# Layer 1's linear attention: one raw projection of queries and keys, with the four taps moved from TensorE to ScalarE, GpSimd and VectorE

## The reference, cut to what matters

```python
def short_conv(x, w):                       # w: 128 channels x 4 taps
    xp = jnp.pad(x, ((0, 0), (3, 0), (0, 0)))
    y = x
    for j in range(4):
        y = y + xp[:, j:j + l, :] * w[:, j]
    return y
q = l2norm(silu(short_conv(x @ Wq.T, conv_q)))      # 16 heads of 8
k = l2norm(silu(short_conv(x @ Wk.T, conv_k)))
v = silu(short_conv(x @ Wv.T, conv_v))
# per head: o = q @ W_init + causal(q @ k.T) @ v, normalised over the head's 8 channels
return (layernorm(o) * gamma + beta) * (x @ Wg.T) @ Wo.T
```

## Time and profile before

| | us |
|---|---|
| median of 3 runs (3835.6 to 3837.76) | 3836.73 |
| the profiled execution | 3835.66 |
| its span in the profile | 3833.8 |
| TensorE matmul busy over the span | 3465.1 (90%) |
| VectorE busy | 2688.0 (70%) |
| ScalarE busy | 2437.2 (64%) |
| GpSimd busy | 2075.0 (54%) |

### The profile page before, as it was taken

One profiled execution on the slowest core, in us unless ns is written; L12 is line 12 of the kernel. 1 busy time (PEld: TensorE's weight loads), 2 busy tenths in 40 slices (PEclk: granted clock), 3 DMA queues, 4 the chain that ended last, 5 costly groups with the idle time before them and its releaser, 6 DMA issues. The chain is left out here.

```text
span 3833.8 us, 90102 instructions
## 1 busy us (share of the span) xinstructions
PE 3465.1 (90%) x30069; PEld 2574.1 (67%) x30069; DVE 2688.0 (70%) x5870; ACT 2437.2 (64%) x9595; POOL 2075.0 (54%) x2606
## 2 busy tenths in 40 slices
PE   8989979988988999999889998899899998788897
PEld 5656645557776878888666665666688874456587
DVE  6857749977774767777688886644577754979822
ACT  6958944445452437777635991455688875688655
POOL 4534319977993433344366540275666635556744
PEclk9989999999999999999989998999999999999889
DMA  7013420010000000000000003135500003300078
GB/s 110 2 23 48 53 61 1 1 56 1 1 1 22 2 2 7 6 7 6 6 2 6 12 7 119 28 99 91 220 22 21 22 30 116 116 2 10 31 263 302
DMA packets 320103, 185.17 MB, mean 48 GB/s; under 512 B 214104, under 2 KB 289127, under 8 KB 318613
## 3 DMA queue, kind: packets, MB, share of 16 engines
q1 hardware_dynamic: 303716, 147.68, 14.2%
q0 software_dynamic: 13568, 27.36, 3.1%
q10 hardware_dynamic: 2370, 4.39, 0.3%
HBM read 131.43 MB, written 50.54 MB: 47 GB/s over the span
## 5 line engine op out<-in xcount | busy, mean ns | idle before, releaser
L3889 POOL DMA_INDIRECT l2f_b_xb<-l2f_tokens,l2f_inv x160 | 155.5, 972 | 174.8 <-issue 157.9
L2684 POOL TENSOR_TENSOR l1x_Sx<-l1x_Sx,l1x_sm 128x512 f32<-128x512 f32 x128 | 132.6, 1046 | 184.7 <-DVE l1x_sm L2890 184.7
L2684 POOL TENSOR_TENSOR l3a_Sx<-l3a_Sx,l3a_sm 128x512 f32<-128x512 f32 x128 | 133.4, 1043 | 129.8 <-DVE l3a_sm L2890 128.2
L3005 ACT ACTIVATE l1x_Sx<-l1x_Sx,l1x_nmx 128x128 f32<-128x128 f32 x512 | 199.0, 393 | 3.8 <-DVE l1x_nmx L2884 3.8
L1470 PEld LDWEIGHTS l0f_acc<-l0f_d_xk,l0f_d_Z 128*128 128x128 f32 x1024 | 124.7, 191 | 113.8 <-POOL l0f_d_Z L1438 112.8
L3005 ACT ACTIVATE l3a_Sx<-l3a_Sx,l3a_nmx 128x128 f32<-128x128 f32 x512 | 199.0, 392 | 0.1
L865 ACT ACTIVATE l3f_Pr<-l3f_S,l3f_nmx 128x128 f32<-128x128 f32 x512 | 182.5, 402 | 3.3 <-DVE l3f_nmx L795 3.3
L865 ACT ACTIVATE l2x_Pr<-l2x_S,l2x_nmx 128x128 f32<-128x128 f32 x512 | 183.9, 426 | 0.4 <-DVE l2x_nmx L795 0.4
L1350 ACT ACTIVATE l0x_Pr<-l0x_S,l0x_nmx 128x128 f32<-128x128 f32 x512 | 181.4, 403 | 3.1 <-DVE l0x_nmx L1267 2.6
L865 ACT ACTIVATE l0a_Pr<-l0a_S,l0a_nmx 128x128 f32<-128x128 f32 x512 | 182.6, 406 | 0.7 <-DVE l0a_nmx L795 0.7
L1470 PE MATMUL l0f_acc<-l0f_d_xk,l0f_d_Z 128*128 128x128 f32 x1024 | 144.5, 284 | 25.1 <-POOL l0f_d_Z L1438 24.9
(11 more groups left out here) (757 smaller groups left out, 11938.7 us busy)
## 6 DMA issues: line engine op xcount, KB each, us to landing
l3f_b_W<-in_l3f_we SPq DMA_DIRECT2D x72, 514.0 KB, 5.5
l3f_sorted<-l3a_blank SPq DMA_DIRECT2D x1, 17680.0 KB, 51.1
l3x_Mb<-l3x_dram_max SPq DMA_DIRECT2D x32, 512.0 KB, 4.3
l2f_results<-l2f_b_ys SPq DMA_DIRECT2D x40, 256.0 KB, 2.8
l2f_W<-in_l2f_w SPq DMA_DIRECT2D x1, 6144.0 KB, 25.9
l3f_b_xb<-l3f_sorted SPq DMA_DIRECT2D x72, 65.0 KB, 4.4
l0f_ew<-in_l0f_ew SPq DMA_DIRECT2D x1, 4096.0 KB, 13.2
l3f_XS<-l3f_results SPq DMA_DIRECT2D x8, 512.0 KB, 6.6
```

The lines of the kernel that those rows point to most:

```text
L2684: pool.tensor_tensor(quad(Sx, s, q), quad(Sx, s, q), bcast_in(sm[:, s, 4 * q:4 * q + 4], P), ALU.mult).then_inc(w_done, 1)
L3005: ins = nc.scalar.activation(Sx[:, s, h, :], Sx[:, s, h, :], ACT.Exp, bias=nmx[:, s, h:h + 1], accum_out=sm[:, s, h:h + 1])
L3889: pool.indirect_dma_start(xb[:, j % 16, :], None, rows[:, :], bass.IndirectOffsetOnAxis(inv[:, j:j + 1], 0), bounds_check=None).then_inc(x ...
```

## The change

The queries and keys are projected once, raw, by one matmul each, from the unshifted block. ScalarE then reads each result from PSUM four times, scaling by a per-channel column (`cols[:, n, j]`, the tap) and writing at a shift of 3-j tokens to `terms`: eight activations for each block, four for the queries (`scale_terms(b, 0)`) and four for the keys (`scale_terms(b, 1)`). GpSimd adds terms 0 and 1 to terms 2 and 3 in one instruction of 128x512 (`pair_terms`); VectorE adds the two halves in one of 128x256 (`convolve`); and `silu_qk` reads the sum from SBUF. Values and gate are projected as before. The pipeline becomes deeper: LayerNorm runs for b+6, `apply` for b+5, `normed_T` and `copy_normed` for b+4, the projection for b+3, and the loop over steps begins at -6. `xb` has three buffers, and bank A comes free at `scaled`. A small DMA brings the tap columns `l1a_cc`, and one small VectorE instruction adds 1 to the last tap.

```diff
-    xb = sb("xb", [P, 2, 3 + P])
+    xb = sb("xb", [P, 3, 3 + P])
+    terms = sb("terms", [P, 4, 2, P])
+    cv = sb("cv", [P, 2, 2, 2, P])
...
+        def pair_terms(b):
+            wait(pool, scaled, b + 1)
+            wait(pool, qkt_done, b - 1)
+            if b == 0:
+                wait(pool, zeros_done, 1)
+            pool.tensor_tensor(cv[:, b % 2, :, :, :], terms[:, 0:2, :, :], terms[:, 2:4, :, :],
+                               ALU.add).then_inc(pairs_done, 1)
...
             if span(b - 2):
                 gated(b - 2)
-            if span(b + 4):
-                wait(pool, ln.done, b + 3)
-                ln.rstd(pool, b + 4, b % 2, C)
-                ln.offset(pool, b + 4, b % 2)
+            if span(b + 3):
+                pair_terms(b + 3)
+            if span(b + 6):
+                wait(pool, ln.done, b + 5)
+                ln.rstd(pool, b + 6, b % 2, C)
+                ln.offset(pool, b + 6, b % 2)
...
         def project_qk(b, n):
-            wait(pe, xb_done, b + 1)
-            wait(pe, qkt_done, b)
+            wait(pe, xb_done, min(b + 2, NB))
+            wait(pe, scaled, b)
             if b == 0:
                 wait(pe, zeros_done, 1)
-            cols = slice(n * P, (n + 1) * P)
-            for j in range(4):
-                mm = nc.tensor.matmul(A[:, cols], taps[:, j, cols], xb[:, b % 2, j:j + P],
-                                      start=(j == 0), stop=(j == 3))
+            mm = nc.tensor.matmul(A[:, n * P:(n + 1) * P], (wq, wk)[n], xb[:, b % 3, 3:3 + P], start=True, stop=True)
...
         def normed_T(b):
             wait(pe, ln.done, b + 1)
-            wait(pe, qkt_done, b)
+            wait(pe, scaled, b - 1)
...
             if span(b - 2):
                 turn_scale(b - 2)
+            if span(b + 4):
+                normed_T(b + 4)
             if span(b - 1):
                 sum_keys(b - 1)
-            if span(b + 2):
-                project_qk(b + 2, 0)
+            if span(b + 3):
+                project_qk(b + 3, 0)
             if span(b - 1):
                 centre(b - 1)
-            if span(b + 2):
-                project_qk(b + 2, 1)
+            if span(b + 3):
+                project_qk(b + 3, 1)
...
-            if span(b + 3):
-                normed_T(b + 3)
...
+        def convolve(b):
+            wait(dve, pairs_done, b + 1)
+            nc.vector.tensor_tensor(cv[:, b % 2, 0, :, :], cv[:, b % 2, 0, :, :], cv[:, b % 2, 1, :, :],
+                                    ALU.add).then_inc(conv_done, 1)
...
                 mask(b, 1)
-            if span(b + 4):
-                wait(dve, ln.offset_done, b + 3)
-                ln.moments_of(nc, dve, b + 4, b % 2, X)
+            if span(b + 2):
+                convolve(b + 2)
+            if span(b + 6):
+                wait(dve, ln.offset_done, b + 5)
+                ln.moments_of(nc, dve, b + 6, b % 2, X)
...
+        def scale_terms(b, n):
+            wait(act, qk_mm, b + 1)
+            wait(act, pairs_done, b)
+            if b == 0:
+                wait(act, zeros_done, 1)
+            for j in range(4):
+                ins = nc.scalar.activation(terms[:, j, n, 3 - j:P], A[:, n * P:n * P + P - 3 + j], ACT.Identity,
+                                           scale=cols[:, n, j:j + 1])
+            if n == 1:
+                ins.then_inc(scaled, 1)
...
         def silu_qk(b):
             wait(act, pv_mm, b - 3)
             wait(act, qexp_done, b - 3)
-            wait(act, qk_mm, b + 1)
-            nc.scalar.activation(qkT[:, b % 4, :], A[:, 0:2 * P], ACT.Silu).then_inc(qkt_done, 1)
+            wait(act, conv_done, b + 1)
+            nc.scalar.activation(qkT[:, b % 4, :], cv[:, b % 2, 0, :, :].rearrange("p n t -> p (n t)"), ACT.Silu).then_inc(qkt_done, 1)
...
         def copy_normed(b):
-            wait(act, vg_mm, b - 1)
+            wait(act, vg_mm, b - 2)
...
             if span(b - 2):
                 copy_scale(b - 2)
-            if span(b + 3):
-                ln.apply(nc, act, b + 3, (b + 3) % 2, X, xnt_mm)
+            if span(b + 4):
+                copy_normed(b + 4)
+            if span(b + 5):
+                ln.apply(nc, act, b + 5, (b + 1) % 2, X, xnt_mm)
...
                 square_centred(b - 1)
+            if span(b + 3):
+                scale_terms(b + 3, 0)
             if span(b + 2):
                 silu_qk(b + 2)
                 silu_v(b + 2)
             if span(b + 3):
-                copy_normed(b + 3)
+                scale_terms(b + 3, 1)
...
+                sp.dma_start(cc[:, :, :], d["l1a_cc"]).then_inc(w_in, 16)
...
-                dve.wait_ge(w_in, 64)
+                dve.wait_ge(w_in, 80)
+                nc.vector.tensor_scalar(cc[:, :, 3], cc[:, :, 3], 1.0, 0.0, ALU.add, ALU.add)
```

More of the change, by code:

```diff
@@ L1904, in stage_l0_ffn, with delta_attention @@
         combine_slots(nc, C, sems, "l0f_c", X, XT, phiX, val)
-def delta_attention(nc, C, sems, x, tag, X, taps, wg, woT, w0, affine):
+def delta_attention(nc, C, sems, x, tag, X, wq, wk, cols, taps, wg, woT, w0, affine):
     sb = lambda n, shape: x.enter_context(nc.sbuf_tensor(f"{tag}_{n}", shape, F32))
     ln = LayerNorm(nc, sb)
-    xb = sb("xb", [P, 2, 3 + P])
+    xb = sb("xb", [P, 3, 3 + P])
+    terms = sb("terms", [P, 4, 2, P])
+    cv = sb("cv", [P, 2, 2, 2, P])
     qkT = sb("qkT", [P, 4, 2 * P])
@@ L1931, in delta_attention @@
      v_done, qexp_done, s_mm, p_done, pv_mm, ot_done, cen_mm, osq_done, rt_mm, rt_done, u_done,
-     wide_done, g_done, y_mm, x_done) = sems(27)
+     wide_done, g_done, y_mm, x_done, scaled, pairs_done, conv_done) = sems(30)
     ln.sems(sems)
@@ L2035, in project_v @@
             for j in range(4):
-                nc.tensor.matmul(B[:, 0:P], xb[:, b % 2, j:j + P], taps[:, j, 2 * P:3 * P],
+                nc.tensor.matmul(B[:, 0:P], xb[:, b % 3, j:j + P], taps[:, j, 2 * P:3 * P],
                                  start=(j == 0), stop=(j == 3))
-            nc.tensor.matmul(B[:, P:2 * P], wg, xb[:, b % 2, 3:3 + P], start=True, stop=True).then_inc(vg_mm, 1)
+            nc.tensor.matmul(B[:, P:2 * P], wg, xb[:, b % 3, 3:3 + P], start=True, stop=True).then_inc(vg_mm, 1)
         def normed_T(b):
             wait(pe, ln.done, b + 1)
-            wait(pe, qkt_done, b)
+            wait(pe, scaled, b - 1)
             nc.tensor.transpose(A[:, 2 * P:3 * P], ln.xn[:, b % 2, :], C.ident).then_inc(xnt_mm, 1)
@@ L2129, in vector @@
         nc.vector.memset(xb[:, :, 0:3], 0.0)
+        nc.vector.memset(terms[:, 0:3, :, 0:3], 0.0)
         nc.vector.memset(Vx[:, :, :], 0.0).then_inc(zeros_done, 1)
@@ L2171, in copy_normed @@
         def copy_normed(b):
-            wait(act, vg_mm, b - 1)
+            wait(act, vg_mm, b - 2)
             wait(act, xnt_mm, b + 1)
-            nc.scalar.copy(xb[:, b % 2, 3:3 + P], A[:, 2 * P:3 * P]).then_inc(xb_done, 1)
+            nc.scalar.copy(xb[:, b % 3, 3:3 + P], A[:, 2 * P:3 * P]).then_inc(xb_done, 1)
         def step(b):
@@ L2194, in delta_attention @@
                  gpsimd=gpsimd, tensor=tensor, vector=vector, scalar=scalar, S=S, x_done=x_done,
-                 banks={"S0": ((p_done, 2 * NB - 1),), "S1": ((p_done, 2 * NB),), "A": ((qkt_done, NB), (xb_done, NB)),
+                 banks={"S0": ((p_done, 2 * NB - 1),), "S1": ((p_done, 2 * NB),), "A": ((scaled, NB), (xb_done, NB)),
                         "B": ((vs_done, NB),), "O": ((ot_done, NB), (x_done, NB)), "Y": ((u_done, NB), (rt_done, NB), (osq_done, NB), (r_done, NB + 2))})
@@ L3140, in stage_l1_l2_attns @@
         gb = sy("l1a_gb", [P, 2])
+        cc = sy("l1a_cc", [P, 2, 4])
         with nc.psum_tensor("l1a_idle", [P, 512], F32) as idle, nc.psum_tensor("l1x_pb", [P, 512], F32) as pb, \
@@ L3192, in stage_l1_l2_attns @@
         at = len(sems.used)
-        delta = delta_attention(nc, C, sems, y, "l1a", X, taps, w1[:, 3, :], w1[:, 4, :], w0, gb)
+        delta = delta_attention(nc, C, sems, y, "l1a", X, w1[:, 0, :], w1[:, 1, :], cc, taps, w1[:, 3, :], w1[:, 4, :], w0, gb)
         delta_sems = sems.used[at:]
@@ L3222, in _ @@
                 steps = delta.gpsimd(pool), wide.gpsimd(pool), phi.gpsimd(pool), heads.gpsimd(pool)
-                for n in range(-4, HEADS + NB + 2):
+                for n in range(-6, HEADS + NB + 2):
                     steps[0](n)
@@ L3249, in _ @@
                 hold_clock(nc, C, delta.S, 3)
-                for n in range(-3, HEADS + NB + 2):
+                for n in range(-6, HEADS + NB + 2):
                     steps[0](n)
@@ L3301, in _ @@
                 steps = delta.scalar(act), wide.scalar(act), phi.scalar(act), heads.scalar(act)
-                for n in range(-4, HEADS + NB + 1):
+                for n in range(-6, HEADS + NB + 1):
                     steps[0](n)
@@ L4634, in arrange @@
     a["l1a_conv"] = np.concatenate([v["L1_attn_conv_" + n] for n in "qkv"]).T.reshape(-1)
+    a["l1a_cc"] = cols([v["L1_attn_conv_" + n].reshape(P, 4) for n in "qk"])
     blocks = np.zeros((16, 8, 16, 8), np.float32)
```

## The result

| | before | after |
|---|---|---|
| median, us (lowest to highest, runs) | 3837.24 (3835.6 to 3838.83, 4) | 3907.09 (3903.55 to 3909.99, 4) |
| profiled execution, its span | 3835.66, 3833.8 | 3909.99, 3908.2 |
| GpSimd busy over the span | 2075.0 (54%) | 2117.6 (54%) |
| ScalarE busy over the span | 2437.2 (64%) | 2503.3 (64%) |

The changed kernel is slower: ratio 1.018, 95% interval 1.0168 to 1.0193. The forecast of 3881 was 26 us short, and 3907.09 lies above the range's 3903.

A forecast was written before the change was run, and what follows sets the result against it. A new ring ScalarE-GpSimd-ScalarE was to set the block at 8.26 us. Fill 29.0, 26 blocks 214.8, then 6.8 and three of 6.4 sum to 269.8 against 224.3: 45.5 us more, so 3881 us, range 3855 to 3903.

The forecast's parts named there:

- The ring from ScalarE's end through `pair_terms`, LayerNorm and `apply`: New ring of one block, ScalarE to GpSimd and back to ScalarE's last term: 8.26 us, between 7.5 and 8.7.
- the first part: From ScalarE's last term to `apply`: hand-overs 0.06 each, `pair_terms` 1.33, LayerNorm's four 1.41; in all 2.86 us.
- the next ring, through normed_T: `normed_T(b+4)` behind turn_scale waits for the previous step's last terms, with sum_keys queued behind it: 6.9 us.
- The removed matmuls: Queries' and keys' projection on TensorE: 1.33 us a block saved, of which only 0.59 could reach the end.
- matrix work sets the block: Rival: TensorE decides, not the rings; 29 blocks x 1.33 = 39 less, fill 5 more: 3802 us, chance 0.04.
- The rival in which LayerNorm's wait doesn't bind: Offsets are ready earlier, the 6.9 us ring decides, the fill adds 3 to 5: 3840 us, chance 0.06.
- The terms: ScalarE's four activations with one column each, read from PSUM: 1.14 us a run, bounds 0.70 and 1.6.
- The estimate of 1.26 for four: Skill page's figure for four terms on ScalarE, 0.29 each, giving a ring of 8.4; the forecast used 1.14 instead.
- the clock: TensorE: PE busy about three quarters of each block, wait of some 1.5 us for copy_out, 2.4 GHz expected.
- a rival, with half of the blocks slow: Half of the blocks at 1.2 GHz, squares to gate doubled: 16 x 1.8 = 29 more, 3910 us; fallen clock's chance 0.08.
- the fill: Stage's start: first terms at about 6, both groups 8.2, steps -2 to 0 of 6.5 each, Silu table 1.28: 29.0 us.
- `convolve` "costs nothing": VectorE, between mask and moments: some 0.4 us, covered by 1.50 us of idle ahead of `add`.

The follow-up runs named there:

- e2: The changed kernel with LayerNorm's four instructions ahead of `pair_terms` on GpSimd instead of behind it: 3852.31 us, ratio 1.0044.
- e7: The changed kernel with one activation for the keys' terms in place of four from block 1 on: 3871.33 us.
- e3: The kernel before with one projection matmul in place of four for queries and for keys, nothing put in their place: 3819.31 us, ratio 0.9952.
- e1: The changed kernel with idle matmuls in TensorE's waits, five behind the queries' projection and one behind the keys': 3891.96 us, ratio 1.0143.
- e4: The changed kernel with the keys' four terms ahead of `silu_v` on ScalarE instead of behind it: 3865.82 us, ratio 1.0082.
- e5: The changed kernel with LayerNorm's four ahead of `pair_terms` on GpSimd and the keys' terms ahead of `silu_v` on ScalarE: 3862.52 us, ratio 1.0069.
- e6: The changed kernel with two idle matmuls behind the queries' projection and none behind the keys': 3900.63 us.
- e9: e5 with the pairs issued a step later on GpSimd, behind `unit_keys`, where VectorE masks: 3832.8 us, ratio 1.0.
- e8: e5 with one Silu activation on a single column in the setup, to load the table early: 3858.11 us, ratio 1.0056.
- e10: The kernel before with an unused 128x512 addition on buffers of its own ending GpSimd's step: 3856.6 us.
- e11: e10 with a `memset` of 128x1024 in place of the addition: 3834.66 us.

## Why the prediction was wrong, by its steps

- **The sign and the mechanism were right.** The ring from ScalarE's end through `pair_terms`, LayerNorm and `apply` sets the block: 8.36 against 8.26, each of its five parts within 0.10. Inside the first part LayerNorm's four took 1.55 us against 1.41, and the pairs 1.23 up to LayerNorm's start against 1.33. Taking LayerNorm out of it (e2) gives 6.88, where the forecast had the next ring, through normed_T, at 6.9; shortening the terms (e7) shortens the block by as much.
- **The removed matmuls** were worth 0.59 a block, as put (e3). With that the rival "matrix work sets the block" falls: 5.6 us was reached by no kernel. The rival in which LayerNorm's wait doesn't bind falls with e2.
- **The terms** took 1.16 for four (forecast 1.14), the pairs 1.28 alone (1.33). The estimate of 1.26 for four, from the Trainium skill's page "ScalarE: Activation LUTs", section "What ACT_TABLE_LOAD costs", was further off; the measurement decides.
- **The step that failed is the clock:** "My blocks are busier than both, so I expect 2.4 GHz." At full clock they had PE busy for 6.40 of 8.36 us, and the granted clock still fell to half behind the waits, over and over: 0.88 over 25 blocks, 16.1 us, removed by e1 with nothing but idle matmuls. The forecast itself named a clock below 1.00 as a sign that it was wrong. It held this as a rival, with half of the blocks slow, at 3910 and a chance of 0.08; 3907 was measured. That time is nearly the measured one by luck: the price was too high, 29 us against 16.1 (16 times 1.8, where 15 falls cost 1.1 each), by about as much as other terms were too low. Its chance was far too small. The two windows of the earlier trace rows that it went by are of this stage's tail and of layer 3, with the waits laid out in another way, and a mean over a window says nothing of where in it the waits lie.
- **Two terms were mis-sized:** the ring by 0.10 us a block and two somewhat longer blocks, 209.4 - 206.5 = 2.9 by e1's 25 blocks; the fill by 2.1 (39.4 against 37.3). With the clock, 16.1 + 2.9 + 2.1 = 21.1 of the 26 us. At the end of the stage nothing was lost. Of the remaining 5, 1.6 are the profiled execution of before against its median (3837.24 - 3835.66); the other 3 were not placed, and single executions differ by as much ahead of the stage and behind it.
- **`convolve` "costs nothing"** holds in the changed kernel, where VectorE idles 2.73 us ahead of `add`, more than the 1.50 of the earlier trace rows, and even in e2, where it takes 0.93 us and 0.73 of idle time are left. But the forecast looked for room in time only, and not for what GpSimd does meanwhile. In the changed kernel that was harmless (L2117 keeps its 0.17 us); in e4 and e5 `pair_terms` fell on the roots and cost a block 1.0 us.

What stays open: what exactly makes the granted clock fall. e1's filling held it, a third of it in e6 did not. The length of the waits alone does not sort the kernels: in e5 TensorE waited 1.10 us for the roots and 0.20 for square in blocks of 7.50, and the clock stayed at 1.00; in e7 it waited 1.13 us for copy_out and 0.20 for square in blocks of 7.56, and had 0.93. No run tells the two apart.

## What to carry to other kernels

Ahead of moving work onto an engine, write down each queue in order and ask what is queued behind the new instruction's wait: here four tiny instructions behind a 1.28 us addition closed a ring worth 37 us, and a swap undid it. Then look at what the new instruction runs beside: on VectorE's roots it cost 1.0 us a block, beside the mask nothing. Look up first what the removal alone is worth on the present ring (0.59 us a block, not 1.33); the pipeline's extra steps cost their 8 us once, against some 12 won in e9. And once a block has waits on TensorE, price a fallen clock and give it more than a small chance: of the kernels here whose TensorE waits for about 1 us or more in most blocks, the changed one, e6 and e7 lost the clock, e4, e5 and e8 did not.

## What the runs showed of the hardware

- **GpSimd holds some of VectorE's instructions.** Beside a 128x512 addition of two streams on GpSimd, a 128x16 instruction of two SBUF inputs took 1.21 us instead of 0.18 and ended 0.04 us behind it (e5; back at 0.18 in e9, where the addition lies elsewhere). A TENSOR_SCALAR with one SBUF input took 0.64 instead of 0.18 (e10), and 0.45 beside a memset (e11). In these the held instruction ends as GpSimd's ends, so its price is the rest of GpSimd's instruction; the 128x256 `convolve` ended 0.28 us behind (e2). The Trainium skill, page "GPSIMD Engine Reference", section "8. Key points", says that GpSimd shares its SBUF interfaces with VectorE and contends with VectorE's instructions in a 2-port mode or with two SBUF inputs; e5's rows agree, and for the one-input L2094 no row shows which mode it ran in.
- **Others run beside it at their own length.** With one input from PSUM, the mask took 1.23 us beside the addition (e9), the `add` 0.29 and L2092 0.18 inside it (e10). Beside the memset, an instruction with two SBUF inputs kept its 0.19 us (e11).
- **The clock fell behind waits of 1.5 us.** TensorE at 2.4 GHz, which waited 1.50 and 0.20 us in each block of 8.36, was granted 1.2 GHz for most of the four us from 1317 on in the next block, and 15 times in 25 blocks. With idle matmuls in the waits, 0.39 and 0.20 us of them left, it stayed at 2.4 GHz over 209.43 us (e1).
